# Gated recurrence: the merges of the blocks' inverses on GpSimd, with sums by halving additions

## The chip, the cores and the metric

The kernel runs on 1 core of one Trainium2 chip. The metric is the device time of one execution in microseconds (us); the time before is the median of 3 runs. The engines are TensorE (PE in the profile), VectorE (DVE), ScalarE (ACT), GpSimd (POOL) and SyncE (SP). Each runs its own list of instructions in order and waits for the others by semaphores.

## The reference

The program is a network of four layers with three sublayers each, on a state of 64 sequences x 32 steps x 128 features in float32. The change is in one sublayer, `_L1_attn_ref`, a gated recurrence with 16 heads of width 64:

```
def step(carry, inp):
    S, R = carry
    kn = k_t / max(norm(k_t), 1e-12)
    r = clip(v_t - S^T kn, -1, 1)
    S = a_t * S;   S = S + b_t * kn (v_t - S^T kn)^T
    o = S^T q_t
    R = aR_t * R;  R = R + g_t * kn (r - R^T kn)^T
    o = o + R^T q_t
```

`S` and `R` are 64 x 64 states for each sequence and head, `a`, `aR`, `b`, `g` are sigmoids of projections of the input, and the sequence has T = 32 steps. All `o` go through an output projection and are added to the state of the network.

## The kernel before

Twelve sublayers run one after the other (`program`, with a barrier between); `l1_attn` is the fifth of them. It doesn't step through time. For each sequence and head the recurrence is a triangular system over the 32 steps, I + L, with L built from products of keys, gates and betas. The kernel works on 16 tiles (`NT`) of 128 columns, 4 sequences x 32 steps each.

- TensorE builds the matrices of S and R in 5 levels (`fill_s`, `fill_r`, L3096). Between two levels VectorE scales rows and columns by the gates' products (`advance`, L3354 to L3362, operands in SBUF) and takes the results from PSUM by masked copies (`keep_s`, `keep_r`).
- The 32 x 32 system is inverted as two diagonal blocks of 16. ScalarE gathers the needed entries of `ms` and `mr` into `kc` (`gather`, L2927 and L2928). VectorE turns `kc` by 32 x 32 transposes into `lt` (`turn`, L3451), so that each partition holds one matrix, and sets the first off-diagonal of the inverse `xi` to minus that of `lt` (L3452). `merge(2)`, `merge(4)` and, for each of the two blocks of 16, `merge_last(n)` join pairs of inverted blocks: two batched small products, each an elementwise product into `tmp` with stride-0 and swapped operands (L3464, L3468, L3482, L3484) and a sum over the last axis (`tensor_reduce`, L3466, L3470, L3483, L3485). The minus sign sits in the second sum. `turn_back` (L3488) transposes `xi` back into `kc`, and ScalarE spreads it into `wideX` (`widen_x`).
- TensorE applies the inverses in a chain of steps per tile (`step_y`, `step_z`, `step_u`, `step_p`, `step_y2`, `step_z2`, `step_wr`, `step_o`, `step_out`), with copies by ScalarE between them; VectorE clips (`clip`, L3495) and adds the result (`result`, L3501).

The order on each engine is written out by hand in a loop of 18 rounds. In round i tile i is built (`now`), tile i-1 inverted (`mid`), tile i-2 applied (`old`) and tile i+1 projected (`new`). Round 1 has the first inversion and nothing to apply, round 16 the last inversion and no more building. In VectorE's list the pieces of the inversion stand among the levels: turn after the first advance, merge(2) after level 1 of S, merge(4) after level 1 of R, merge_last(0) after level 2, merge_last(1) after level 3, then `norms(i + 1)` (L3306 to L3308, which TensorE's `broadcast`, L3086, waits for), turn_back, the last level of S, and `keys(i + 1)`. In round 16 the order is turn, the merges with `result(13)` between merge(4) and merge_last, turn_back, clip. TensorE's `step_y(14)` waits for semaphore `x`, which `result(13)` raises. GpSimd does some memsets and the first residual of this sublayer and is idle for the rest of it.

`Steps` is a helper that lets an instruction raise a semaphore and its own engine wait for it before the next one.

## Time and profile before

| | |
|---|---|
| runs before, us | 3167.33 median (3166.45 to 3175.26) |
| profiled execution, us | 3174.15, span 3172.3 |
| TensorE busy | 2612.6 us (82%) |
| VectorE busy | 2138.2 us (67%) |
| ScalarE busy | 1425.9 us (45%) |
| GpSimd busy | 567.4 us (18%) |
| the sublayer, from its first fills to its last result | about 930 to 2066 us |

The profile is one execution. Busy time of an engine is the time in which an instruction of it ran. The view of waits says for each instruction how long its engine stood idle before it, and whose event ended that; "issue" is idle time for which the profile shows no releaser. The time in a row of the timeline is that of the whole merged group. Most of the span lies in other sublayers, which the change doesn't touch.

### The profile page before, as it was taken

How to read it: one execution, taken by the hardware profiler on the slowest of the kernel's cores; microseconds unless marked ns; L12 is line 12 of the kernel's file. 1: busy time of each engine (PE TensorE's matmuls, PEld its weight loads, DVE VectorE, ACT ScalarE, POOL GpSimd, SP SyncE). 2: the span in 40 equal slices, each digit the busy share in tenths (PEclk: the TensorE clock that was granted, in tenths of full speed). 3: DMA queues.
4: the chain of work that ended last, by engine and by line, in shares of the span. 5: the costliest groups of instructions: out<-in, count | busy, mean ns of one | idle time of the engine just before them, and what ended most of it. 6: DMA issues, size and time to landing. Idle time of an engine off the chain costs nothing. (4 is left out here: it accounts for less than half of the span.)

```text
span 3172.3 us, 120225 instructions
## 1 busy us (share of the span) xinstructions
PE 2612.6 (82%) x52165; PEld 1926.9 (61%) x52187; DVE 2138.2 (67%) x5457; ACT 1425.9 (45%) x3330; POOL 567.4 (18%) x592
## 2 busy tenths in 40 slices
PE   8977478999976788888888887769999997787735
PEld 5645365555656667676776776547776554575633
DVE  3348335777749889887988889267777666565742
ACT  4342233444453445444554443457776454464310
POOL 0000434555530000000000000010000441261025
PEclk9879687999988899999998999879999998798865
DMA  3200331111110000000000000000101003152013
GB/s 89 58 9 14 104 126 50 44 44 53 42 52 4 4 4 4 4 4 4 4 4 4 4 4 4 2 16 25 27 25 54 3 4 102 45 117 64 5 51 104
DMA packets 69932, 109.63 MB, mean 35 GB/s; under 512 B 10336, under 2 KB 55024, under 8 KB 68880
## 3 DMA queue, kind: packets, MB, share of 16 engines
q1 hardware_dynamic: 57776, 80.34, 8.0%
q0 software_dynamic: 11696, 22.40, 2.9%
q8 instruction: 382, 6.26, 0.8%
q14 instruction: 78, 0.64, 0.1%
HBM read 90.06 MB, written 16.51 MB: 34 GB/s over the span
## 5 line engine op out<-in xcount | busy, mean ns | idle before, releaser
L3096 PE MATMUL psum<-l1d_rw,l1d_cols 64*32 64x32 f32 (+2 forms) x20480 | 240.0, 215 | 85.9 <-issue 65.6
L3096 PEld LDWEIGHTS psum<-l1d_rw,l1d_cols 64*32 64x32 f32 x20480 | 209.3, 108 | 129.2 <-issue 104.1
L2476 POOL TENSOR_SCALAR l1xs_p<-l1xs_p,l1xs_col 128x257 f32<-128x257 f32 x256 | 233.8, 932 | 204.5 <-DVE l1xs_col L2432 204.5
L2397 ACT ACTIVATE l1xs_p<-psum,l1xs_col 128x257 f32<-128x257 f32 x256 | 119.5, 472 | 209.4 <-DVE l1xs_col L2427 203.1
L1747 POOL TENSOR_SCALAR X<-X,l1f_bias 128x512 f32<-128x512 f32 x4 | 6.3, 1589 | 1144.3 <-DMA l1f_bias<-in_l1f_bias 1144.3
L3354 DVE TENSOR_TENSOR l1d_rw<-l1d_rw,l1d_tots 128x1536 f32<-128x1536 f32 x96 | 143.2, 1491 | 72.6 <-PE psum L3096 71.6
L2870 ACT COPY l1d_ya<-psum 128x512 f32<-128x512 f32 x160 | 92.8, 590 | 197.9 <-PE psum L3136 196.7
L2439 DVE STREAM_TRANSPOSE l1xs_pt<-l1xs_p 128x288 f32<-128x288 f32 x256 | 122.4, 478 | 78.6 <-POOL l1xs_p L2476 78.5
L2692 ACT ACTIVATE l2x_p<-psum,l2x_top 128x257 f32<-128x257 f32 x256 | 120.5, 474 | 58.3 <-PE psum L2605 46.0
L3033 PE MATMUL psum<-l1d_src,l1d_wp 128*128 128x128 f32 x1024 | 138.5, 292 | 2.7 <-ACT l1d_src L2875 1.3
L2349 PE MATMUL psum<-l1xs_keys,l1xs_qx 128*32 128x257 f32 x2048 | 134.3, 396 | 3.5 <-DVE l1xs_qx L2421 1.9
L2361 PE MATMUL psum<-l1xs_pt,l1xs_vals 32*128 32x512 f32 x1152 | 136.6, 604 | 0.0
L3033 PEld LDWEIGHTS psum<-l1d_src,l1d_wp 128*128 128x128 f32 x1024 | 127.6, 203 | 7.0 <-issue 3.7
L2605 PE MATMUL psum<-consts,l2x_p 128*86 128x128 f32 x768 | 120.6, 280 | 1.7 <-ACT l2x_p L2692 1.1
L2734 DVE TENSOR_REDUCE l2x_top<-psum 128x1 f32<-128x257 f32 x256 | 96.9, 420 | 36.8 <-PE psum L2594 33.1
L1993 POOL TENSOR_TENSOR l2a_phi<-l2a_pos,l2a_ex 128x512 f32<-128x512 f32 x64 | 79.9, 1270 | 128.9 <-ACT l2a_ex L1979 128.9
L2427 DVE TENSOR_REDUCE l1xs_col<-psum 128x1 f32<-128x257 f32 x256 | 101.0, 409 | 2.7 <-PE psum L2349 2.6
L2605 PEld LDWEIGHTS psum<-consts,l2x_p 128*86 128x86 f32 x768 | 78.8, 122 | 33.4 <-issue 23.1
L3086 PE MATMUL psum<-l1d_small,l1d_hsel 32*128 32x384 f32 x256 | 67.0, 661 | 37.5 <-DVE l1d_small L3308 28.3
L2349 PEld LDWEIGHTS psum<-l1xs_keys,l1xs_qx 128*32 128x32 f32 x2048 | 61.9, 111 | 53.9 <-issue 24.7
L2330 PEld LDWEIGHTS psum<-XN,l1x_wqk 128*128 128x128 f32 x512 | 66.1, 202 | 46.9 <-issue 32.6
L2590 PE MATMUL psum<-l2x_keys,l2x_qx 32*128 32x257 f32 x512 | 90.1, 433 | 3.4 <-DMA l2x_mask<-l2x_table 3.4
(558 smaller groups left out, 6742.8 us busy)
## 6 DMA issues: line engine op xcount, KB each, us to landing
l2f_w<-in_l2f_w SPq DMA_DIRECT2D x16, 768.0 KB
l1xs_vals<-in_ctx_strips SPq DMA_DIRECT2D x16, 576.0 KB
l0x_ctxT<-in_ctxT SPq DMA_DIRECT2D x16, 516.0 KB, 3.7
l1xs_keys<-in_ctxT SPq DMA_DIRECT2D x16, 516.0 KB
l2x_ctxT<-in_ctxT SPq DMA_DIRECT2D x64, 129.0 KB, 2.1
l1d_wp<-in_l1d_wp SPq DMA_DIRECT2D x1, 2048.0 KB, 8.1
l2f_acc<-l2f_zero SPq DMA_DIRECT2D x8, 256.0 KB, 3.6
l2f_sums<-l2f_acc SPq DMA_DIRECT2D x8, 256.0 KB, 3.5
```

The lines of the kernel that those rows point to most:

```text
L2349: mm = nc.tensor.matmul(score_ps(t)[32 * c:32 * c + 32, :S2], qx[:, g % 2, n, 32 * c:32 * c + 32], keys[:, g % 2, c, :S2], start=True, sto ...
L2361: mm = nc.tensor.matmul(u_ps[c][:], vals[r, g % 2, j, :], pt[r, g % 2, :, j, :], start=(j == 0), stop=(j == STRIP - 1))
L2397: nc.scalar.activation(p[:, t % 4, :S2], score_ps(t)[:, :S2], ACT.Exp, bias=col[:, 0, t % 4:t % 4 + 1], accum_out=col[:, 1, t % 4:t % 4 + ...
L2427: nc.vector.tensor_reduce(col[:, 0, t % 4:t % 4 + 1], score_ps(t)[:, :S2], AX.X, ALU.max, negate=True).then_inc(s["mx"], 1)
L2439: nc.vector.transpose(pt[:, g % 2, n].rearrange("p j r -> p (j r)"), p[:, t % 4, :]).then_inc(s["pt"], 1)
L2476: nc.gpsimd.tensor_scalar(p[:, t % 4, :S2], p[:, t % 4, :S2], col[:, 2, t % 4:t % 4 + 1], None, ALU.mult).then_inc(s["norm"], 1)
L2605: mm = nc.tensor.transpose(t_ps[j % 2][:KC, c * 128:(c + 1) * 128], p[:, j, c * KC:(c + 1) * KC], k.const("ident"))
L2692: nc.scalar.activation(p[:, j, :S2], s_ps[j][:, :S2], ACT.Exp, bias=top[:, l % 2, j:j + 1], accum_out=sums[:, l % 2, j:j + 1]).then_inc(s[ ...
L2734: nc.vector.tensor_reduce(top[:, l % 2, j:j + 1], s_ps[j][:, :S2], AX.X, ALU.max, negate=True).then_inc(s["mx"], 1)
L3033: mm = nc.tensor.matmul(k.ps[into + j][:, e * 128:(e + 1) * 128], wp[:, n, c:c + 128], src[:], start=True, stop=True)
L3096: mm = nc.tensor.matmul(k.ps[bank0 + pr + e // per * 2][b * T:b * T + T, e % per * w:(e % per + 1) * w], cols[rr, 2 * n, e * 128 + b * T:e ...
L3354: tt(x, x, over.to_broadcast([128, feats.stop - feats.start, 32 * (16 >> lv), m]), ALU.mult)
```

## The change

The three merge functions move from VectorE's list to GpSimd's. GpSimd waits for `turn`, then does merge(2), merge(4) and merge_last for both blocks, whose instructions now alternate; two halves of `tmp` and of `wmat` keep the two blocks apart. Each `tensor_reduce` is replaced by additions that halve the last axis: one for 2, two for 4, three for 8 elements. The last addition of a merge writes straight into `xi`. The minus sign is taken in ScalarE's gathering: `kc` now holds the negated entries (`nc.scalar.mul` by -1.0 in place of `copy`), so the negated sums and the multiplication by -1 in `turn` fall away. `turn_back` waits for a new semaphore that GpSimd's last additions raise. The rest of VectorE's list keeps its order.

```
--- before.py
+++ after.py
@@ -2791,7 +2791,7 @@
     names = ("src", "srcv", "k_mm", "k", "q_mm", "q", "gate_mm", "gate", "nb_mm", "nb", "small", "bc_mm", "kn", "v_mm", "v",
              "rowS", "rowR", "mS_mm", "mS", "mR_mm", "mR", "kc", "back", "wideM", "wideX", "y_mm", "y", "z_mm", "t", "u_mm",
              "u", "p_mm", "r", "y2_mm", "y2", "z2_mm", "t2", "wr_mm", "wr", "o_mm", "o", "out_mm", "x", "zero", "diag",
-             "norm", "turn", "steps", "resid", "colr", "kr")
+             "norm", "turn", "steps", "resid", "colr", "kr", "merged", "last", "inverse")
     s = {n: k.sem("l1d_" + n) for n in names}
     with ph:
         sb = lambda n, shape, dt=F32: k.sb("l1d_" + n, shape, dt, ctx=ph)
@@ -2823,7 +2823,7 @@
         wideM, wideX = sb("wideM", [128, 5, H, 64]), sb("wideX", [128, 2 * H, 64])
         v, u, rd, ya = (sb(n, [128, 1024]) for n in ("v", "u", "rd", "ya"))
         kc, lt, xi = sb("kc", [128, T * T]), sb("lt", [128, T * (T + 1)]), sb("xi", [128, T * (T + 1)])
-        tmp, wmat = sb("tmp", [128, 1024]), sb("wmat", [128, 64])
+        tmp, wmat = sb("tmp", [128, 1024]), sb("wmat", [128, 128])
         block = ph.enter_context(nc.Block())
 
         def rows(first, last, lv):
@@ -2855,6 +2855,69 @@
             nc.gpsimd.memset(wideM[:], 0.0).then_inc(s["zero"], 1)
             pool.wait_ge(s["zero"], 2)
             nc.gpsimd.memset(xi[:, 0:T * T:T + 1], 1.0).then_inc(s["zero"], 1)
+            tt = nc.gpsimd.tensor_tensor
+
+            def blocks(x, m):
+
+                return (x.rearrange("p (n x) -> p n x", x=2 * m * (T + 1))[:, :, :2 * m * T]
+                        .rearrange("p n (r c) -> p n r c", c=T))
+
+            def merge(i, m):
+
+                nb, lb, xb = T // (2 * m), blocks(lt, m), blocks(xi, m)
+                lo, hi = slice(0, m), slice(m, 2 * m)
+                t5 = tmp[:, :nb * m * m * m].rearrange("p (n r c k) -> p n r c k", n=nb, r=m, c=m)
+                w4 = wmat[:, :nb * m * m].rearrange("p (n r c) -> p n r c", n=nb, r=m)
+                flat = tmp[:, :nb * m * m * m].rearrange("p (x k) -> p x k", k=m)
+                right = lambda x: x.rearrange("p n k c -> p n c k")
+                left = lambda x, r: x[:, :, r:r + 1, :].to_broadcast([128, nb, m, m])
+                step = Steps(pool, s["merged"], i, 10, {2: 0, 4: 4}[m])
+                for r in range(m):
+                    ins = tt(t5[:, :, r], left(lb[:, :, hi, lo], r), right(xb[:, :, lo, lo]), ALU.mult)
+                step(ins)
+                if m == 4:
+                    step(tt(flat[:, :, :2], flat[:, :, :2], flat[:, :, 2:], ALU.add))
+                step(tt(wmat[:, :nb * m * m], flat[:, :, 0], flat[:, :, 1], ALU.add))
+                for r in range(m):
+                    ins = tt(t5[:, :, r], left(xb[:, :, hi, hi], r), right(w4), ALU.mult)
+                step(ins)
+                if m == 4:
+                    step(tt(flat[:, :, :2], flat[:, :, :2], flat[:, :, 2:], ALU.add))
+                step(tt(xb[:, :, hi, lo], t5[:, :, :, :, 0], t5[:, :, :, :, 1], ALU.add))
+
+            def merge_last(i):
+
+                m = 8
+                lb, xb = blocks(lt, m), blocks(xi, m)
+                lo, hi = slice(0, m), slice(m, 2 * m)
+                w4 = [wmat[:, 64 * n:64 * n + 64].rearrange("p (r c) -> p r c", r=m) for n in range(2)]
+                t4 = [tmp[:, 512 * n:512 * n + 512].rearrange("p (r c k) -> p r c k", r=m, c=m) for n in range(2)]
+                flat = [tmp[:, 512 * n:512 * n + 512].rearrange("p (x k) -> p x k", k=m) for n in range(2)]
+                left = lambda x: x.unsqueeze(2).to_broadcast([128, m, m, m])
+                right = lambda x: x.rearrange("p k c -> p c k").unsqueeze(1).to_broadcast([128, m, m, m])
+                for part_ in range(8):
+                    for n in range(2):
+                        if part_ > 0:
+                            pool.wait_ge(s["last"], i * 14 + 2 * part_ + n - 1)
+                        if part_ == 0:
+                            ins = tt(t4[n], left(lb[:, n, hi, lo]), right(xb[:, n, lo, lo]), ALU.mult)
+                        elif part_ == 4:
+                            ins = tt(t4[n], left(xb[:, n, hi, hi]), right(w4[n]), ALU.mult)
+                        elif part_ in (1, 5):
+                            ins = tt(flat[n][:, :, :4], flat[n][:, :, :4], flat[n][:, :, 4:], ALU.add)
+                        elif part_ in (2, 6):
+                            ins = tt(flat[n][:, :, :2], flat[n][:, :, :2], flat[n][:, :, 2:4], ALU.add)
+                        elif part_ == 3:
+                            ins = tt(wmat[:, 64 * n:64 * n + 64], flat[n][:, :, 0], flat[n][:, :, 1], ALU.add)
+                        else:
+                            ins = tt(xb[:, n, hi, lo], t4[n][:, :, :, 0], t4[n][:, :, :, 1], ALU.add)
+                        ins.then_inc(s["inverse" if part_ == 7 else "last"], 1)
+
+            for i in range(NT):
+                pool.wait_ge(s["turn"], 2 * i + 2)
+                merge(i, 2)
+                merge(i, 4)
+                merge_last(i)
 
         @block.scalar
         def _(act):
@@ -2924,8 +2987,8 @@
                 if i > 0:
                     act.wait_ge(s["wideX"], i)
                 at = kc[:].rearrange("p (t c) -> p c t", t=T)
-                copy(at[:, :H, :], ms[:, i % 2, :, 0, :])
-                copy(at[:, H:, :], mr[:, i % 2, :, 1, :]).then_inc(s["kc"], 1)
+                nc.scalar.mul(at[:, :H, :], ms[:, i % 2, :, 0, :], -1.0)
+                nc.scalar.mul(at[:, H:, :], mr[:, i % 2, :, 1, :], -1.0).then_inc(s["kc"], 1)
 
             def widen(i, j):
 
@@ -3438,53 +3501,16 @@
                         ins = vc.copy_predicated(ll[:, i % 2, 1, hs[pr], :], top, part_[:, :, 1, :])
                 ins.then_inc(s["mR"], 1)
 
-            def blocks(x, m):
-
-                return (x.rearrange("p (n x) -> p n x", x=2 * m * (T + 1))[:, :, :2 * m * T]
-                        .rearrange("p n (r c) -> p n r c", c=T))
-
             def turn(i):
 
                 dve.wait_ge(s["kc"], i + 1)
                 t = Steps(dve, s["turn"], i, 2)
                 first = lambda x: x[:, T:T * T:2 * (T + 1)]
                 t(vc.transpose(lt[:, :T * T], kc[:]))
-                t(vc.tensor_scalar(first(xi), first(lt), -1.0, None, ALU.mult))
-
-            def merge(m):
-
-                nb, lb, xb = T // (2 * m), blocks(lt, m), blocks(xi, m)
-                lo, hi = slice(0, m), slice(m, 2 * m)
-                t5 = tmp[:, :nb * m * m * m].rearrange("p (n r c k) -> p n r c k", n=nb, r=m, c=m)
-                w4 = wmat[:, :nb * m * m].rearrange("p (n r c) -> p n r c", n=nb, r=m)
-                flat = tmp[:, :nb * m * m * m].rearrange("p (x k) -> p x k", k=m)
-                right = lambda x: x.rearrange("p n k c -> p n c k")
-                left = lambda x, r: x[:, :, r:r + 1, :].to_broadcast([128, nb, m, m])
-                for r in range(m):
-                    ins = tt(t5[:, :, r], left(lb[:, :, hi, lo], r), right(xb[:, :, lo, lo]), ALU.mult)
-                step(ins)
-                step(vc.tensor_reduce(wmat[:, :nb * m * m], flat, AX.X, ALU.add))
-                for r in range(m):
-                    ins = tt(t5[:, :, r], left(xb[:, :, hi, hi], r), right(w4), ALU.mult)
-                step(ins)
-                step(vc.tensor_reduce(wmat[:, :nb * m * m], flat, AX.X, ALU.add, negate=True))
-                step(vc.tensor_copy(xb[:, :, hi, lo], w4))
-
-            def merge_last(n):
-
-                m = 8
-                lb, xb = blocks(lt, m), blocks(xi, m)
-                lo, hi = slice(0, m), slice(m, 2 * m)
-                w4 = wmat[:, :m * m].rearrange("p (r c) -> p r c", r=m)
-                t4 = tmp[:, :512].rearrange("p (r c k) -> p r c k", r=m, c=m)
-                left = lambda x: x.unsqueeze(2).to_broadcast([128, m, m, m])
-                right = lambda x: x.rearrange("p k c -> p c k").unsqueeze(1).to_broadcast([128, m, m, m])
-                step(tt(t4, left(lb[:, n, hi, lo]), right(xb[:, n, lo, lo]), ALU.mult))
-                step(vc.tensor_reduce(w4, t4, AX.X, ALU.add))
-                step(tt(t4, left(xb[:, n, hi, hi]), right(w4), ALU.mult))
-                step(vc.tensor_reduce(xb[:, n, hi, lo], t4, AX.X, ALU.add, negate=True))
+                t(vc.tensor_copy(first(xi), first(lt)))
 
             def turn_back(i):
+                dve.wait_ge(s["inverse"], 2 * i + 2)
                 vc.transpose(kc[:], xi[:, :T * T]).then_inc(s["back"], 1)
 
             def clip(i):
@@ -3523,13 +3549,9 @@
                     advance_r(i, 0)
                     advance_s(i, 1)
                     keep_s(i, 1)
-                if mid:
-                    merge(2)
                 if now:
                     advance_r(i, 1)
                     keep_r(i, 1)
-                if mid:
-                    merge(4)
                 if i == NT:
                     result(i - 3)
                 if now:
@@ -3540,15 +3562,11 @@
                     keep_s(i, 2)
                     advance_r(i, 2)
                     keep_r(i, 2)
-                if mid:
-                    merge_last(0)
                 if now:
                     advance_s(i, 3)
                     keep_s(i, 3)
                     advance_r(i, 3)
                     keep_r(i, 3)
-                if mid:
-                    merge_last(1)
                 if new:
                     norms(i + 1)
                 if mid:
```

## Rows read from the trace of the kernel before

**Rows 1.** Busy time by stretch (columns in its first line, x = instructions)
```profile
core 0: us, PE busy (x) PEld busy (x) DVE busy (x) ACT busy (x) POOL busy (x), PEclk, DMA share, GB/s
1003.00:1068.00 65.00, 40.94 (x1596) 32.82 (x1598) 63.63 (x131) 26.51 (x53) 0.00 (x0) 0.82 0.01 3
...
1390.00:1455.00 65.00, 55.97 (x1987) 45.59 (x1987) 56.88 (x119) 31.23 (x62) 0.00 (x0) 0.92 0.02 4
```

**Rows 2.** Who waited for whom, TensorE, 1130 to 1910 us
```profile
PE psum L3096 <- issue: 41.6, 43, 2.2
...
PE psum L3086 <- DVE l1d_small L3308: 17.2, 11, 2.2
```

**Rows 3.** The same view and stretch, VectorE
```profile
DVE l1d_rw L3354 <- PE psum L3096: 57.5, 41, 3.7
```

**Rows 4.** One stretch, instructions on tile tmp alone
```profile
1399.60:1442.80 43.20, 10.49 (x24) 1.00 0.02 4
```

**Rows 5.** Groups of instructions on GpSimd, all of the span
```profile
L2476 POOL TENSOR_SCALAR l1xs_p<-l1xs_p,l1xs_col 128x257 f32<-128x257 f32 x256 | 233.8, 932 | 204.5 <-DVE l1xs_col L2432 204.5
...
L1993 POOL TENSOR_TENSOR l2a_phi<-l2a_pos,l2a_ex 128x512 f32<-128x512 f32 x64 | 79.9, 1270 | 128.9 <-ACT l2a_ex L1979 128.9
...
L2552 POOL TENSOR_TENSOR l2x_qx<-l2x_q,consts 128x128 f32<-128x128 f32 x64 | 25.5, 398 | 330.6 <-PE psum L2594 294.4 <-DVE l2x_q L2727 36.2
...
L2857 POOL MEMSET l1d_xi<- 128x32 f32 x1 | 0.2, 154 | 0.1
```

**Rows 6.** In order of time, VectorE, one middle tile; start us, us, then instruction
```profile
1399.45 0.18 DVE L3452 TENSOR_SCALAR l1d_xi<-l1d_lt 128x16 f32<-128x16 f32 x1
...
1441.19 0.23 DVE L3306 TENSOR_SCALAR l1d_small<-l1d_small 128x128 f32<-128x128 f32 x1
...
1442.78 1.24 DVE L3488 STREAM_TRANSPOSE l1d_kc<-l1d_xi 128x1024 f32<-128x1024 f32 x1
```

**Rows 7.** The same stretch as rows 4, line L3354 alone
```profile
1399.60:1442.80 43.20, 10.19 (x7) 1.00 0.02 4
```

**Rows 8.** The same stretch, line L3356 alone
```profile
1399.60:1442.80 43.20, 4.77 (x7) 1.00 0.02 4
```

**Rows 9.** The page's costliest groups
```profile
L2870 ACT COPY l1d_ya<-psum 128x512 f32<-128x512 f32 x160 | 92.8, 590 | 197.9 <-PE psum L3136 196.7
...
L3086 PE MATMUL psum<-l1d_small,l1d_hsel 32*128 32x384 f32 x256 | 67.0, 661 | 37.5 <-DVE l1d_small L3308 28.3
```

**Rows 10.** Who waited for whom, TensorE, 930 to 1003 us
```profile
PE psum L3086 <- DVE l1d_small L3308: 3.0, 2, 2.5
```

**Rows 11.** The same view, 1003 to 1068 us
```profile
PE psum L3086 <- DVE l1d_small L3308: 6.1, 1, 6.1
```

**Rows 12.** In order of time, ScalarE, middle tile
```profile
1439.45 0.28 ACT L2918 ACTIVATE l1d_small<-psum 128x128 f32<-128x128 f32 x1
```

**Rows 13.** In order of time, TensorE, middle tile
```profile
1437.42 2.08 PE L3136 MATMUL psum<-l1d_ya,l1d_wideX 64*64 64x64 f32 x64
...
1441.38 0.36 PE L3096 MATMUL psum<-l1d_rw,l1d_cols 64*32 64x48 f32 x21 [0.76 <-issue]
...
1442.92 1.52 PE L3086 MATMUL psum<-l1d_small,l1d_hsel 32*128 32x384 f32 x8 [1.18 <-DVE l1d_small L3308]
```

**Rows 14.** In order of time, VectorE, the last tile
```profile
1993.12 0.18 DVE L3452 TENSOR_SCALAR l1d_xi<-l1d_lt 128x16 f32<-128x16 f32 x1
...
1997.56 0.29 DVE L3501 TENSOR_TENSOR X<-X,psum 128x128 f32<-128x128 f32 x1
...
2014.88 0.69 DVE L3495 TENSOR_SCALAR l1d_rd<-psum 128x512 f32<-128x512 f32 x1 [8.59 <-PE psum L3136]
```

**Rows 15.** In order of time, TensorE, the last tile
```profile
1997.94 3.68 PE L3136 MATMUL psum<-l1d_v,l1d_wideX 64*64 64x64 f32 x64 [5.85 <-issue]
```

**Rows 16.** Groups of instructions on ScalarE, all of the span
```profile
L2927 ACT COPY l1d_kc<-l1d_ms 128x512 f32<-128x512 f32 x16 | 18.0, 1124 | 0.0
...
L620 ACT ACTIVATE l0a_sc<-psum 128x512 f32<-128x512 f32 x16 | 8.6, 610 | 6.5 <-PE psum L527 6.5
```


## The prediction

> **What bounds the kernel now.** The change touches one stage of twelve, the gated recurrence, which runs from about 930 to 2066 us of the span; all else keeps its time. I read the stage in this order: busy time by stretch, who waits for whom, one tile in order of time, and then the two ends of the loop.
>
> The windows show two regimes. In the tile 1003 to 1068 us VectorE is busy 63.6 of 65 us and TensorE 40.9, so VectorE sets the pace. In a tile of the middle both are near the top, TensorE 56.0 and VectorE 56.9 of 65 [rows 1]. Busy shares alone don't say which of two engines leads; the waits do. Over 1130 to 1910 us VectorE waited 57.5 us at L3354 for TensorE's fills [rows 3], while TensorE's waits that name VectorE are led by 17.2 us for the key norms (`small`, L3308) [rows 2]. TensorE's largest idle is the 41.6 us "issue" in the fills, gaps in the middle of a run of matmuls that no engine caused [rows 2]. So TensorE leads in the middle tiles, VectorE runs just behind it, and a lighter VectorE can give back only those places where TensorE stands waiting for it.
>
> **The merges leave VectorE.** In the middle tile the instructions that touch `tmp` took 10.5 us [rows 4]; with the two copies into `xi` and the hand-offs I take 11 us a tile (estimate). This is the most that a tile can win, and only where VectorE leads.
>
> **The merges on GpSimd.** Per tile, from the diff: merge(2) has 6 instructions of 32 elements; merge(4) 10 of 64 and 2 of 128; merge_last 4 each of 512, 256, 128 and 64. GpSimd's tensor_tensor took 1270 ns for 512 elements and 398 ns for 128 [rows 5]. The line through both is 108 ns + 2.27 ns an element, which gives 181 ns for 32, 253 for 64, 689 for 256. The sum is 1.1 + 3.3 + 10.4 = 14.8 us. Some 24 of the 34 instructions wait for the one before; the one such wait in the trace cost 0.1 us (last column of the memset L2857) [rows 5], so 2.4 us more: 17.3 us from turn to last merge. The rows have no strided or broadcast operand on GpSimd. As an upper bound I take its dearest rate per element, 932 ns for 257 [rows 5], 3.2 ns, and 0.3 us a wait: 20 + 7 = 27 us. As a lower bound, 15 us. I take 17.3, because the nearest row is the same operation.
>
> Is it hidden? In the middle tile `turn` ends at 1399.63 and `turn_back`, which now waits for GpSimd, starts at 1442.78 [rows 6]. It would start at about 1441.4 (below), so 41.7 us are free. What stands behind turn_back on VectorE is the last take of S, the next tile's keys, and behind these TensorE's broadcasts: a late GpSimd would stop everything. At 17 or 27 us it isn't late.
>
> **Both engines at once.** No row shows a GpSimd operation beside a VectorE operation with two SBUF inputs; I bound it. At best nothing. At worst one holds the other off for each whole instruction. VectorE's `advance` lines with two SBUF inputs take 10.2 and 4.8 us between turn and turn_back [rows 7, 8]. Added whole to GpSimd's chain that is 17.3 + 15.0 = 32.3 us, still under 41.7. VectorE would in turn wait for remains of GpSimd instructions, on average under 0.5 us each for 14 advances and fewer while GpSimd is busy: 0 to 6 us a tile. In the middle tiles this has cover: 11 us of merges are gone, and VectorE waited for the fills anyway. In the tile where VectorE leads it counts. I take 5 us there.
> The Trainium skill, "SBUF — State Buffer", section "Who interferes with whom", speaks against the change: a VectorE instruction with two SBUF inputs and a GpSimd instruction that reads SBUF take turns on one read interface, and the one that comes later is blocked for the whole instruction. By that rule the worst case above is the true one, with the sum as I give it; without it the tile that VectorE leads would win 5 us more. No row of before has both kinds side by side.
>
> **Middle tiles: the wait for the norms.** The page has 28.3 us of TensorE waiting at L3086 for `small` [rows 9]; 3.0 us of it lie before the first merge [rows 10] and 6.1 in the VectorE-led tile [rows 11], which leaves 19.2 us for 13 tiles. In the tile shown, ScalarE's square root ended at 1439.73 [rows 12], but VectorE began the norms only at 1441.19, after merge_last [rows 6]. Without the merge the norms begin 1.46 us earlier. TensorE waited 1.18 us [rows 13], so here all goes. In tiles without an issue gap ahead of it the wait was longer and a remainder stays, since ScalarE and the norms alone outlast TensorE's 2.08 us of step_wr and its fill: about 0.5 us, the tiles without merges show the same kind. So 19.2 - 13 x 0.5 = 12.7 us. What is late next is TensorE's own "issue" gap, as the 0.76 us before this very wait [rows 13]: if instructions are what comes late, a removed wait in part becomes such a gap. I take off 2.7: **10 us** (bounds 0 to 19).
>
> **The VectorE-led tile.** 11 us leave VectorE, contention returns 5: **6 us** (bounds 0 to 11). TensorE allows it: it waited 6.1 us there for the norms [rows 11] and its 40.9 us busy leave room [rows 1]. The tile after it may give 1.
>
> **The last tile.** Here GpSimd's chain is bare. Before, VectorE ends turn at 1993.30, does merge(2) and merge(4), and only then `result` at 1997.56 [rows 14]; TensorE's next step starts at 1997.94 after 5.85 us of idle that the profile calls issue, but step_y waits for just this result (`x`) [rows 15]. After the change result follows turn at once: 4.2 us earlier. But the clip that TensorE needs later (2014.88) now stands behind turn_back, and that behind GpSimd: 1993.3 + 17.3 + 1.25 for the transpose = 2011.9. So the end moves by 2014.88 - 2011.9 = **3 us** (bounds +4 to -7, the latter for a chain of 27).
>
> **ScalarE's sign and the rest: 0.** The gathering copy of 512 elements took 1124 ns [rows 16], strided in its output; the same multiply by a constant took 610 ns dense [rows 16], where the dense COPY took 590 (ya, on the page) [rows 9]. 20 ns each is nothing, ends +-0.2 us a tile, and it lies ahead of turn with room except once at the end. tensor_copy for tensor_scalar on 16 elements: 0. The third wait of `turn_back` costs what is said above.
>
> Sum: 10 + 6 + 1 + 3 = 20 us. The profiled execution took 3174.15 us (span 3172.3), so 3154 for its like. That execution lies 6.8 us above the median of 3167.33, and the same 20 us off the median give **3147 us**.
>
> **Rivals.**
> *A, the supply of instructions rules (chance 0.2).* For: 41.6 us of issue gaps, the largest wait of TensorE, in nearly every tile. Against: in most tiles no gap follows the norms. Then the 10 us shrink to 2 and the led tile gives 3; with the 3 at the end, 8 us: 3159, no change that can be told.
> *B, GpSimd is late for turn_back (0.1), the other sign.* It decides once chain plus contention passes 41.7 us; from there each microsecond costs one in each of 14 tiles. For: nothing shows GpSimd's rate on broadcast, strided operands. At its upper bound, 27 + 15 = 42 us, it only just decides; at 45 (a chain of 30) it costs 3.3 x 14 = 46, and at the bare end 30 - 20.3 = 10 more, with the norms' gain kept (10): 3167 + 46 = 3213. Against: the chain would have to be 1.6 times mine, with all the contention on top.
> *C, more comes free (0.12).* No contention, so the led tile gives 11, the norms 15, and the shorter idle at the end lets the step there, 3.68 us [rows 15], take the 2.08 of the same step in the middle tile [rows 13]: some 32 us with 1 of the tile after the led one: 3135.
> *D, nothing is freed in the led tile and the chain is 25 us (0.08).* VectorE is slowed by as much as it was relieved: 10 + 0 - 5 = 5 us: 3162.
> The forecast holds the remaining 0.5.
>
> **Numbers.** About 0.3%, 9.5 us, is what can be told from no change. Faster by more: forecast (most of it) and C and a part of A: 0.66. Within: rest of A, D: 0.22. Slower: B and the worst of D: 0.12. Range 3126 to 3174, which holds A, C and D, with the far end of B outside. The profiled executions may scatter as the runs before did (3166.45 to 3175.26).
>
> **What would show it.** The lines of the merges stand under POOL with about 17 us a tile, 240 to 280 us in all, 512-element products near 1.27 us alone; above 1.4 us beside VectorE they are held off. The advances' mean (1.75 us for 1536 elements in the trace of before) grows if VectorE is held off. TensorE's wait for `small` falls from 28 to about 10 us, VectorE's busy in the middle tile from 57 to about 46, and its waits for TensorE rise by as much. VectorE's wait at turn_back is nil but in the last tile, where it is 15 us or more. If the issue gaps grow by what the wait for `small` lost, A is right; if turn_back waits in the middle tiles, B. Wrong altogether: TensorE's idle in the middle tiles unchanged with a lighter VectorE, or a stage longer than before.

## The result, and the profile after

The changed kernel takes 3152.41 us (median of 15 runs, 3136.83 to 3166.28) and the kernel before, run between them on the same chip, 3169.91 us (15 runs, 3157.01 to 3187.12). The ratio, taken between neighbouring runs and not between the two medians, is 0.9936 with a 95% interval of 0.9914 to 0.9958: 20.3 us faster by the ratio, 17.5 between the medians. Forecast were 20 us and 3147 us, with a range of 3126 to 3174; the 3147 stood on a median of 3167.33 from three runs, which fifteen runs put 2.6 us higher. The profiled execution took 3154.11 us, its span 3152.2 us.

The page's first row (busy time, share of the span, instructions) says what moved: GpSimd 567.4 us before, 957.4 after; VectorE 2138.2 before, 2044.7 after.

```profile
PE 2617.1 (83%) x52187; PEld 1929.1 (61%) x52187; DVE 2044.7 (65%) x5041; ACT 1426.2 (45%) x3330; POOL 957.4 (30%) x1136
```

390 us came to GpSimd and only 93.5 left VectorE. The rest of this text is about that disproportion and about where the 20 us lie.

The stage from its first `turn` to its last `result` took 1057.3 us before and 1038.5 after: 18.8 us less. I cut it at the starts of the turns: the led tile (the one in which VectorE leads, first to second turn), the next tile, the middle (third to fifteenth turn, 12 tiles), the tile ahead of the end, and the end (last turn to last result). The windows of the kernel before, with the columns of [rows 1], led tile and middle:

```profile
1007.80:1065.20 57.40, 36.69 (x1405) 29.00 (x1406) 56.13 (x117) 24.61 (x49) 0.00 (x0) 0.79 0.01 3
1135.20:1937.35 802.15, 688.35 (x23831) 560.72 (x23826) 698.69 (x1430) 386.05 (x741) 0.00 (x0) 0.93 0.02 4
```

The kernel after: led tile, middle, and one middle tile that answers to the second of [rows 1]:

```profile
1009.40:1063.40 54.00, 36.66 (x1405) 29.11 (x1406) 52.04 (x92) 24.64 (x49) 27.33 (x34) 0.84 0.02 4
1130.46:1918.74 788.28, 679.25 (x23831) 555.32 (x23826) 630.02 (x1117) 386.36 (x741) 296.35 (x408) 0.95 0.02 4
1389.00:1454.00 65.00, 57.08 (x1995) 46.69 (x1995) 53.51 (x95) 32.98 (x64) 24.82 (x34) 0.95 0.02 4
```

Led tile 57.4 to 54.0, middle 802.15 to 788.28, and over the middle VectorE's busy 698.69 to 630.02. TensorE's own busy time fell as well, 688.35 to 679.25, at a granted clock of .93 before and .95 after, although its matmuls are the same. The waits of TensorE in the middle, before (waiting line, releaser, sum in us, times, longest; the lines are the fills, the broadcast that waits for the norms, and the steps):

```profile
PE psum L3096 <- issue: 41.6, 43, 2.2
PE psum L3086 <- DVE l1d_small L3308: 18.7, 12, 2.2
...
PE psum L3136 <- issue: 6.6, 10, 1.1
```

and after:

```profile
PE psum L3159 <- issue: 52.5, 51, 2.5
...
PE psum L3199 <- issue: 7.6, 13, 1.3
...
PE psum L3149 <- DVE l1d_small L3371: 3.8, 6, 0.7
```

The wait for the norms fell from 18.7 to 3.8 us, and the issue gaps of fills and steps together rose from 48.2 to 60.1. Last, two groups of VectorE's waits in the stage after: its largest, for TensorE's fills at the advances (71.6 us before), and a new one, for GpSimd at `turn_back`:

```profile
DVE l1d_rw L3417 <- PE psum L3159: 112.7, 51, 5.7
...
DVE l1d_kc L3514 <- POOL l1d_xi L2913: 16.4, 1, 16.4
```

### The profile page after: what moved, and what is told of

It reads as the page before. It is cut to its first block and busy times, and to the rows that moved or that the text cites. A ratio compares the mean times of both kernels' runs of the same rounds, so it can differ in the third digit from the quotient of the medians.

```text
span 3152.2 us, 120361 instructions
## 1 busy us (share of the span) xinstructions
PE 2617.1 (83%) x52187; PEld 1929.1 (61%) x52187; DVE 2044.7 (65%) x5041; ACT 1426.2 (45%) x3330; POOL 957.4 (30%) x1136
## 5 line engine op out<-in xcount | busy, mean ns | idle before, releaser
L2876 POOL TENSOR_TENSOR l1d_tmp<-l1d_lt,l1d_xi 128x64 f32<-128x64 f32 (+1 forms) x96 | 41.7, 463 | 666.0 <-DVE l1d_xi L3510 664.7
L3417 DVE TENSOR_TENSOR l1d_rw<-l1d_rw,l1d_tots 128x1536 f32<-128x1536 f32 x96 | 168.2, 1753 | 112.8 <-PE psum L3159 112.7
L2439 DVE STREAM_TRANSPOSE l1xs_pt<-l1xs_p 128x288 f32<-128x288 f32 x256 | 122.4, 478 | 78.6 <-POOL l1xs_p L2476 78.6
L2552 POOL TENSOR_TENSOR l2x_qx<-l2x_q,consts 128x128 f32<-128x128 f32 x64 | 25.4, 398 | 329.0 <-PE psum L2594 293.9
L3419 DVE TENSOR_TENSOR l1d_cols<-l1d_cols,l1d_tots 128x512 f32<-128x512 f32 x96 | 96.3, 1004 | 0.0
```

Source lines behind the costliest of these rows:

```text
L2439: nc.vector.transpose(pt[:, g % 2, n].rearrange("p j r -> p (j r)"), p[:, t % 4, :]).then_inc(s["pt"], 1)
L3417: tt(x, x, over.to_broadcast([128, feats.stop - feats.start, 32 * (16 >> lv), m]), ALU.mult)
```

## Experiments

Each was run beside the kernel before, whose median was 3173.3 to 3174.4 us in the three groups. Stretches are read from one trace each, and the traced run can lie some way off the median of its kernel (last column of the table below). x1 is the changed kernel once more, so that traces of the same program can be set side by side: how far apart two of them lie bounds what one stretch can tell.

**x1, the changed kernel again.** No edit.

> The changed kernel once more, as the measure for the others of this chip. My theory (TensorE leads, VectorE's merges held up the norms): 20 us under the kernel before, ratio 0.993 to 0.995.

Measured: 3152.96 us, ratio 0.9936 [0.9912, 0.9959]. Led tile 55.3 (54.0 in the first trace), middle 793.33 (788.28), end 72.5 (73.0). The time repeats; the middle scatters by 5 us between these two traces. x4 and x6 change nothing in TensorE's list for the middle, which took 792.9 and 780.8 us there: two single traces of the same middle can lie 12 us apart. The kernel before has one trace, with 802.2 us. That the middle gained doesn't rest on one pair: the eight traces with at most 7 us of waits for the norms and turn_back not late lie at 778.5 to 793.3, all under it, and the two with more work ahead of the norms (x9, x10) at 817.1 and 819.0. x3 and x8 repeat the led tile of before (57.3 and 57.5 for 57.4), x3 and x10 its end (71.2 and 73.3 for 73.2), so the end is good to 2 us.

**x2, no merges at all.**
```diff
-            for i in range(NT):
-                pool.wait_ge(s["turn"], 2 * i + 2)
-                merge(i, 2)
-                merge(i, 4)
-                merge_last(i)
...
-                dve.wait_ge(s["inverse"], 2 * i + 2)
```

> The changed kernel without any merge on GpSimd and without turn_back's wait for it (the inverses are left out, the output is not the reference's). This is the change with neither contention nor a bare chain at the end. Theory: contention costs only where VectorE leads, so the first inverted tile gives 3 to 5 us more than the changed kernel's, the middle tiles nothing, the last tile about 6 (no wait for GpSimd, so no idle of TensorE before step_y2): 9 us under the changed kernel, VectorE's advances back at 1757 and 685 ns. Rival (contention is paid in all tiles): 4.6 us a tile, 50 us or more under the changed kernel.

Measured: 3143.61 us, 0.9918 [0.9891, 0.9945]. The windows of its led tile and middle:

```profile
1009.65:1060.20 50.55, 35.55 (x1405) 28.64 (x1406) 46.13 (x92) 24.69 (x49) 0.00 (x0) 0.86 0.02 4
1126.54:1905.01 778.47, 672.22 (x23864) 551.81 (x23856) 576.46 (x1118) 387.27 (x743) 0.00 (x0) 0.96 0.02 4
```

VectorE's busy time in the led tile is 46.13 us, with the merges on GpSimd it was 52.04, in the same 92 instructions: GpSimd's presence costs VectorE 5.9 us there. The led tile is 3.5 us shorter than in the changed kernel (4.7 than in x1) and the end 7 us. The middle is 10 (15) us shorter, but this is the trace of the fastest of six runs, 16.5 us under their median, and only 2 us shorter than the middle of x6. The medians of x1 and x2 lie 9.3 us apart, and 9 was expected: that little is left to win from the merges, wherever they run.

**x3, no GpSimd: merge_last(1) on VectorE, but ahead of the last advances.** From the kernel before:
```diff
                 if mid:
                     merge_last(0)
+                    merge_last(1)
                 if now:
                     advance_s(i, 3)
...
-                if mid:
-                    merge_last(1)
                 if new:
                     norms(i + 1)
```

> The kernel before, all merges on VectorE, with merge_last(1) moved from after level 3 to right after merge_last(0), so that nothing of the inversion stands ahead of the norms. Theory: the middle tiles' gain is TensorE's wait for the norms alone, so this gets it with no GpSimd at all: the wait for the norms falls from 28 to about 15 us (the led tile keeps its part), 10 us under the kernel before. Rival (what counts is VectorE's total load): no change, since VectorE does the same work.

Measured: 3155.51 us, 0.9941 [0.9919, 0.9964]. VectorE does the same work as before; only its last 3.6 us of merging no longer stand right ahead of the norms. TensorE's waits in the middle:

```profile
PE psum L3096 <- issue: 51.1, 48, 2.5
...
PE psum L3086 <- DVE l1d_small L3308: 4.1, 7, 0.7
```

The wait for the norms goes from 18.7 to 4.1 us and the middle from 802.15 to 790.61, what the whole change reached (788.28 and 793.33). The led tile stays at 57.3. The whole run is 18.9 us under the kernel before where I had expected 10, and x1 21.4, a difference that the intervals don't tell apart. So the gain in the middle comes from where VectorE's work stands and not from the engine that does it.

**x4, clip ahead of turn_back in the last round.** From the changed kernel:
```diff
+                if i == NT:
+                    clip(i - 2)
                 if mid:
                     turn_back(i - 1)
-                if i == NT:
-                    clip(i - 2)
```

> The changed kernel with the clip of tile 14 ahead of the last turn_back, so that it doesn't wait for GpSimd's bare chain. Theory: the clip comes 3.1 us earlier, TensorE's 4.5 us of idle before step_y2 shrinks to about 1.3, and the two steps behind it take 2.1 and 2.0 us in place of 3.7 and 3.8: 6 us under the changed kernel, seen between the last turn and the last result (73.0 before, 67 now). Rival (the end is bound by ScalarE's copies or the matmuls themselves): 0 to 3 us.

Measured: 3148.69 us, 0.9924 [0.9899, 0.995], 4.3 us under x1 by the medians, which the intervals don't tell apart; the end took 65.5 us against 73.0 and 72.5, 7 us less where 6 were expected. VectorE at the end of the changed kernel (start, duration, wait in brackets):

```profile
1976.20 0.18 DVE L3510 COPY l1d_xi<-l1d_lt 128x16 f32<-128x16 f32 x1
...
1993.55 1.25 DVE L3514 STREAM_TRANSPOSE l1d_kc<-l1d_xi 128x1024 f32<-128x1024 f32 x1 [16.43 <-POOL l1d_xi L2913]
1994.71 1.25 DVE L3521 TENSOR_SCALAR l1d_rd<-psum 128x512 f32<-128x512 f32 x2
```

and in x4:

```profile
1995.55 0.69 DVE L3521 TENSOR_SCALAR l1d_rd<-psum 128x512 f32<-128x512 f32 x1 [13.54 <-PE psum L3199]
1996.48 0.69 DVE L3521 TENSOR_SCALAR l1d_rd<-psum 128x512 f32<-128x512 f32 x1 [0.24 <-PE psum L3199]
1998.86 1.25 DVE L3514 STREAM_TRANSPOSE l1d_kc<-l1d_xi 128x1024 f32<-128x1024 f32 x1 [1.69 <-POOL l1d_xi L2913]
```

The clip no longer stands behind the 16.4 us wait for GpSimd, and turn_back itself waits 1.69 us. TensorE's steps on this path in the kernel before:

```profile
2002.39 3.75 PE L3131 MATMUL psum<-l1d_v,consts 128*128 128x512 f32 x4 [0.77 <-ACT l1d_ya L2870]
...
2016.56 2.08 PE L3136 MATMUL psum<-l1d_rd,l1d_wideX 64*64 64x64 f32 x64 [0.79 <-DVE l1d_rd L3495]
2019.41 1.96 PE L3131 MATMUL psum<-l1d_rd,consts 128*128 128x512 f32 x4 [0.78 <-ACT l1d_ya L2870]
```

in the changed kernel:

```profile
1977.21 2.08 PE L3199 MATMUL psum<-l1d_v,l1d_wideX 64*64 64x64 f32 x64 [0.50 <-issue]
...
1996.02 3.68 PE L3199 MATMUL psum<-l1d_rd,l1d_wideX 64*64 64x64 f32 x64 [4.48 <-DVE l1d_rd L3521]
2000.47 3.75 PE L3194 MATMUL psum<-l1d_rd,consts 128*128 128x512 f32 x4 [0.78 <-ACT l1d_ya L2933]
```

and in x4:

```profile
1997.23 2.08 PE L3199 MATMUL psum<-l1d_rd,l1d_wideX 64*64 64x64 f32 x64 [0.80 <-DVE l1d_rd L3521]
2000.09 1.96 PE L3194 MATMUL psum<-l1d_rd,consts 128*128 128x512 f32 x4 [0.78 <-ACT l1d_ya L2933]
```

The two steps behind the clip take 2.08 and 1.96 us before and in x4, 3.68 and 3.75 us in the changed kernel, where TensorE had stood idle for 4.48 us ahead of them. The windows of the changed kernel around its first and second row above have the granted clock behind the five busy times, 1.00 and then 0.50, that is 2.4 and 1.2 GHz:

```profile
1977.00:1979.50 2.50, 2.08 (x64) 1.97 (x64) 0.11 (x1) 0.75 (x2) 2.17 (x9) 1.00 0.03 7
...
1995.90:1999.80 3.90, 3.68 (x64) 3.49 (x64) 0.06 (x1) 0.64 (x2) 0.00 (x0) 0.50 0.02 4
```

So 3.4 us hung on the idle time, besides the wait itself. The price isn't fixed. Behind the same wait the two steps took 3.21 and 3.67 us in x1 (idle 4.62) and 3.68 and 1.95 in x9 (idle 4.90): the first step paid each time, the second not always. In the kernel before, it was paid at the head of this path, at 1997.94 [rows 15] and 2002.39 (3.68 and 3.75 us); in x3, with 5.84 us of idle at the same place, it was 3.61 and 1.96.

**x5, GpSimd busy, but only writing.** From the changed kernel, in place of the merges:
```diff
-                merge(i, 2)
-                merge(i, 4)
-                merge_last(i)
+                step = Steps(pool, s["last"], i, 25)
+                for n in range(25):
+                    step(nc.gpsimd.memset(tmp[:], 0.0))
+                nc.gpsimd.memset(tmp[:], 0.0).then_inc(s["inverse"], 2)
```

> The changed kernel with 26 memsets of tmp per tile on GpSimd (about 27 us, each waiting for the one before) in place of the merges (which are left out). GpSimd is as busy as in the changed kernel but only writes. Theory (the two engines contend for reading): VectorE's advances are back at the durations of before, 1757 ns for 1536 elements and 685 ns for 512, and the memsets stay at 0.95 us. Rival (any GpSimd work slows VectorE): the 512-element advances stay near 1000 ns.

Measured: 3165.02 us (one run), led tile 53.2, middle 789.93; the end took 80.1 us, since the last tile waits for 26 us of memsets in place of 17 us of merges. VectorE's two-input advances in the whole stage (group, count, sum, mean ns; these two in x5):

```profile
L3418 DVE TENSOR_TENSOR l1d_rw<-l1d_rw,l1d_tots 128x1536 f32<-128x1536 f32 x48 | 84.4, 1757 | 86.1 <-PE psum L3160 86.0
L3420 DVE TENSOR_TENSOR l1d_cols<-l1d_cols,l1d_tots 128x512 f32<-128x512 f32 x96 | 65.8, 685 | 0.0
```

The same in the kernel before (the 1536 group took 1757 ns there too, `COPY_PREDICATED` is the masked copy from PSUM):

```profile
L3356 DVE TENSOR_TENSOR l1d_cols<-l1d_cols,l1d_tots 128x512 f32<-128x512 f32 x96 | 65.8, 685 | 0.0
L3405 DVE COPY_PREDICATED l1d_ms<-l1d_lmask,psum 128x384 f32<-128x384 int32 x96 | 62.9, 722 | 0.0
L3354 DVE TENSOR_TENSOR l1d_rw<-l1d_rw,l1d_tots 128x1024 f32<-128x1024 f32 x48 | 58.8, 1226 | 59.8 <-PE psum L3096 59.4
```

and in the changed kernel:

```profile
L3419 DVE TENSOR_TENSOR l1d_cols<-l1d_cols,l1d_tots 128x512 f32<-128x512 f32 x96 | 96.3, 1004 | 0.0
L3417 DVE TENSOR_TENSOR l1d_rw<-l1d_rw,l1d_tots 128x1536 f32<-128x1536 f32 x48 | 90.8, 1892 | 53.7 <-PE psum L3159 53.7
L3417 DVE TENSOR_TENSOR l1d_rw<-l1d_rw,l1d_tots 128x1024 f32<-128x1024 f32 x48 | 77.4, 1613 | 59.2 <-PE psum L3159 59.0
L3468 DVE COPY_PREDICATED l1d_ms<-l1d_lmask,psum 128x384 f32<-128x384 int32 x96 | 63.1, 724 | 0.0
```

With 26 memsets of 953 ns a tile on GpSimd the advances take what they take with GpSimd idle. With products on GpSimd 512 elements take 1004 ns in place of 685, 1024 take 1613 in place of 1226, 1536 take 1892 in place of 1757, and the masked copies, which read PSUM, 724 in place of 722. So GpSimd's writing costs VectorE nothing here, and what the merges do beyond it, reading, holds VectorE off, in instructions with two operands in SBUF and not in the masked copies. That is the rule of the Trainium skill, "SBUF — State Buffer", section "Who interferes with whom", and these rows agree with it. Single rows spread widely: of the 96 advances of 512 elements in the changed kernel the shortest took 680 ns, the median 789 and the longest 2039. The longest comes near 685 ns and a whole product of 1.5 us; that one always waits out the other to its end isn't shown.

**x6 and x7, a longer chain on GpSimd.** From the changed kernel, with a spare tile:
```diff
                 pool.wait_ge(s["turn"], 2 * i + 2)
+                step = Steps(pool, s["spare"], i, 4)   # x7: 12
+                for _ in range(4):                     # x7: 12
+                    step(tt(spare[:], lt[:, :512], lt[:, 512:1024], ALU.mult))
                 merge(i, 2)
```

> The changed kernel with 4 more products of 512 elements per tile on GpSimd, ahead of the merges, each waited for: 6.4 us bare, about 8 with contention. Theory: the chain of 28 us has 41.7 us of room in the middle tiles, so their pitch doesn't change; the last tile pays 6.4 us and the half-speed steps stay, the first inverted tile pays about 3: 9 us over the changed kernel, ratio about 0.997. Rival (GpSimd's chain is already what turn_back waits for): 8 us in each of 16 tiles, 120 us more.

> The same with 12 more products, 19 us bare and some 22 with contention: a chain of about 50 us against 41.7 us of room. Theory: turn_back now waits for GpSimd by 5 to 8 us in each middle tile, 75 to 110 us in all, and 19 us at the end. This puts a price on the point from which the change would have been a loss. Rival (room is larger, since turn_back's followers have slack of their own): the waits show but the pitch grows by less than half of them.

Measured: x6 3160.93 us, 0.9958 [0.9938, 0.9977]; x7 3207.24 us (one run), 54 more than the changed kernel. In x6 the middle took 780.8 us, the led tile 55.9, the end 78.6: nothing is lost but at the bare end, 6 us of the 8 by which the median lies above x1 (9 expected). In x7 the middle took 813.1, the led tile 66.5 and the end 87.2, and VectorE waited for GpSimd in ten tiles:

```profile
DVE l1d_kc L3518 <- POOL l1d_xi L2914: 51.6, 10, 32.8
```

32.8 us of this lie in the last tile and 18.8 in the nine others, of which six are in the middle, with 9.0 us. There turn_back starts again and again 44.9 us after turn ends, the length of GpSimd's chain, and the waits are 0.5 to 2.5 us. So the room is 42 to 44 us, as [rows 6] gave (41.7). I had expected 75 to 110 us for the middle, from a chain of 50 us; the chain was 44.8 us long, and the middle lost 20 to 25. Of these the waits at turn_back explain less than half. VectorE was busy 705 us, 75 more than in the changed kernel, and TensorE now waited 20.8 us for its masked copies.

**x8, x3 with the end put right, no GpSimd.**
```diff
                 if mid:
                     turn(i - 1)
+                if i == NT:
+                    result(i - 3)
...
+                if i == NT:
+                    clip(i - 2)
                 if mid:
                     turn_back(i - 1)
```
(on top of x3; both are taken out where they stood).

> The kernel before with nothing on GpSimd: merge_last(1) right after merge_last(0) as in the run before, and in the last round result(13) right after turn and the clip ahead of turn_back. Theory: the middle tiles keep the 11 us of that reordering, the end goes from 73 to 66 us, the first inverted tile stays at 57.5: 18 us under the kernel before, as much as the change itself gives. Rival (GpSimd is needed for most of the gain): under 10 us.

Measured: 3153.68 us, 0.9921 [0.989, 0.9952], 19.8 us under the kernel before by the medians (18 expected); the end took 68.9 us, 2.3 to 4.4 less than in the three traces without its edits, where 7 were expected. TensorE there:

```profile
1985.21 2.60 PE L3224 MATMUL psum<-l1d_rd,l1d_wo 128*128 128x128 f32 x16 [2.72 <-ACT l1d_v L2870]
1988.86 3.68 PE L3136 MATMUL psum<-l1d_v,l1d_wideX 64*64 64x64 f32 x64 [1.04 <-issue]
1993.30 3.65 PE L3131 MATMUL psum<-l1d_v,consts 128*128 128x512 f32 x4 [0.77 <-ACT l1d_ya L2870]
```

Here the steps take 3.68 and 3.65 us where they can take 2.08 and 1.96. Ahead of them stand idles of 2.72 and 1.04 us. In x1 the first of them took 2.08 us behind idles of 2.70 and 0.50, in x6 2.94 behind 2.69 and 0.50, so these rows give no idle time from which it begins; this end still pays at its head.

**x9, VectorE loaded again, just ahead of the norms.** From the changed kernel:
```diff
                     keep_r(i, 3)
+                if mid and i < NT:
+                    for _ in range(7):
+                        step(vc.memset(spare[:], 0.0))
```

> The changed kernel with seven memsets of 512 elements (485 ns each, 3.5 us) on VectorE, at the place where merge_last(1) stood, ahead of the norms. They only write, so they don't hold off GpSimd. VectorE still has 7.5 us a tile less than before the change. Theory (only what stands ahead of the norms counts in the middle tiles): TensorE's wait for the norms in the middle goes from 4 back to about 18 us, and the middle tiles lose their gain of 11 us: ratio 0.997 (first tile and end keep theirs). Rival (VectorE's total load counts): a third of the gain lost, 0.995, and the wait stays under 8 us.

Measured: 3184.53 us, 1.0037 [1.0013, 1.0061]: 31.6 us over x1 and 11.3 over the kernel before, where I had expected the gain of the middle to go and the rest to stay (0.997). The seven memsets took 4.5 us a tile, not 3.5, because each waited 0.17 us for the one before, and the wait for the norms came to 27.6 us and not 18. The middle, with VectorE's busy time third:

```profile
1137.72:1954.83 817.11, 695.82 (x23831) 566.40 (x23828) 669.08 (x1202) 386.60 (x741) 296.64 (x408) 0.91 0.02 4
```

```profile
PE psum L3160 <- issue: 41.3, 41, 2.4
PE psum L3150 <- DVE l1d_small L3372: 27.6, 12, 3.2
```

This is the plainest of the experiments. VectorE is busy 669 us here, 30 less than in the kernel before, and yet the middle is 15 us longer: 817.11 against 802.15. Its total load isn't what counts here, but the 4.5 us (before 3.6) that stand between the last advance and the norms.

**x10, the new arithmetic on the old engine.** From the kernel before: halving additions for each tensor_reduce, the sign taken by ScalarE, merges left on VectorE.
```diff
                 step(tt(t4, left(lb[:, n, hi, lo]), right(xb[:, n, lo, lo]), ALU.mult))
-                step(vc.tensor_reduce(w4, t4, AX.X, ALU.add))
+                flat = tmp[:, :512].rearrange("p (x k) -> p x k", k=m)
+                halve(flat, m)
+                step(tt(wmat[:, :m * m], flat[:, :, 0], flat[:, :, 1], ALU.add))
```
(halve adds the upper half of the last axis to the lower until two elements are left; the other sums likewise).

> The kernel before with the other two parts of the change alone: sums by halving additions and the sign taken by ScalarE, all merges still on VectorE. Expected by both: a reduction of 512 elements, 686 ns, becomes additions of 256, 128 and 64 of together about 1 us, and the copies into xi go; VectorE gets about 1.2 us a tile more. Theory: half of that stands ahead of the norms, about 0.3 us in each of 13 tiles, and 1 us in the first: 3 to 6 us slower than before, no change that can be told. Rival (halving or the sign is a gain by itself): 5 us or more under the kernel before.

Measured: 3185.94 us, 1.0044 [1.002, 1.0067]. One merge_last takes 4.37 us against 3.63, and TensorE in the middle:

```profile
PE psum L3096 <- issue: 42.5, 47, 2.4
PE psum L3086 <- DVE l1d_small L3308: 26.0, 12, 3.0
```

0.74 us more ahead of the norms, and the wait for them goes from 18.7 to 26.0: 7.3 us over 12 tiles, 0.61 a tile. Its cost, 12.7 us by the medians and 14 by the ratio, is above the 3 to 6 that I expected: those left out that TensorE's busy time would be longer too, by 11.5 us at a granted clock of .91.

The middle of all traces (us; "norms" is TensorE's wait for `small`, "issue" its issue gaps in fills and steps; "trace" is how far the traced run lies above the median of its kernel):

| | middle | norms | issue | PE busy | clock | led tile | end | trace |
|---|---|---|---|---|---|---|---|---|
| before | 802.2 | 18.7 | 48.2 | 688.4 | .93 | 57.4 | 73.2 | +4.2 |
| changed | 788.3 | 3.8 | 60.1 | 679.3 | .95 | 54.0 | 73.0 | +1.7 |
| x1 | 793.3 | 4.5 | 55.5 | 686.8 | .94 | 55.3 | 72.5 | +14.3 |
| x2 | 778.5 | 4.5 | 54.6 | 672.2 | .96 | 50.6 | 65.6 | -16.5 |
| x3 | 790.6 | 4.1 | 58.7 | 679.2 | .95 | 57.3 | 71.2 | +8.1 |
| x4 | 792.9 | 3.9 | 60.5 | 685.0 | .94 | 56.6 | 65.5 | +3.2 |
| x5 | 789.9 | 4.5 | 61.2 | 675.4 | .95 | 53.2 | 80.1 | one run |
| x6 | 780.8 | 4.5 | 52.8 | 676.9 | .95 | 55.9 | 78.6 | -10.7 |
| x7 | 813.1 | 6.6 | 46.7 | 690.7 | .93 | 66.5 | 87.2 | one run |
| x8 | 788.1 | 4.4 | 57.6 | 681.1 | .94 | 57.5 | 68.9 | +4.9 |
| x9 | 817.1 | 27.6 | 48.2 | 695.8 | .91 | 58.4 | 71.3 | -2.9 |
| x10 | 819.0 | 26.0 | 49.8 | 699.9 | .91 | 60.2 | 73.3 | +7.6 |

## Why the prediction was right, step by step

**The sum was right; three of its four terms were not quite.** 10 + 6 + 1 + 3 was forecast. The two traces of the changed kernel give 14 and 9 in the middle, 3.4 and 2.1 in the led tile, 2.9 and 2.3 in the next, 0.2 and 0.7 at the end: 20 and 14 in all. The tile ahead of the end took 1.7 and 0.3 us more, so the whole stage gave 18.8 and 13.6, where the ratio of the runs gives 20.3 and the medians 17.5 and 21.4. That the total came out so close is in part luck: led tile and end gave 5 to 6 us less than forecast, and the next tile and, in the first trace, the middle gave as much more.

**Middle tiles: mechanism right, make-up mis-sized.** The norms' wait fell by 14.9 us where I had 12.7. "What is late next is TensorE's own issue gap" holds too, and I took off 2.7 for it where the gaps grew by 12 (x1: 7). That is rival A's mechanism, at A's size in the first trace (four fifths of what the norms lost) and at half of what they lost in x1; A's outcome, 2 us for the middle, didn't come. What I had not put in is TensorE's busy time, which fell as well. In three traces of the changed middle (changed, x1, x4) it fell by 9.1, 1.6 and 3.4 us, and TensorE's whole idle time by 4.8, 7.3 and 5.9. Between traces of the same work the busy time scatters by as much as it fell, so how much of the gain is fewer waits and how much is a higher granted clock (.93 before, .94 to .95 after) stays open. x9 and x10 show the same terms the other way round: norms up, issue at its old size, clock .91, busy time up by 7 and 12 us. That the clock follows from the waits is argued from such rows; no run changed the one and held the other. Why an issue gap comes in where a wait went stays open too: the rows before and after only name it "issue".

**The merges leave VectorE: right size, wrong credit.** VectorE's busy time in the middle fell by 5.7 us a tile: 10.2 us of merges (698.7 before, 576.5 in x2, over 12 tiles), where I had 11 with the hand-offs, less 4.5 of contention. The sign that I gave, 57 to about 46 us in the middle tile, left the contention out; it was 53.5. But x3 shows that the middle would have had its gain with the merges still on VectorE, and x9 that VectorE lighter by 30 us is slower if the work stands ahead of the norms. My own step said this ("the norms begin 1.46 us earlier") and I then told the change as an unloading. The unloading as such is worth the led tile, some 2 us, and no more: with GpSimd and without it, x1 (0.9936) and x3 (0.9941), then x4 (0.9924) and x8 (0.9921), are pairs that the intervals don't tell apart.

**The led tile: 6 forecast, 3.4 and 2.1 measured.** VectorE's busy time fell from 56.1 to 52.0, 10.0 us of merges less 5.9 of contention by x2 (11 and 5 forecast), so 4.1 and not 6 were there to win. TensorE takes the rest: its busy time in this tile depends on the clock, 36.7 us at .84 in the changed kernel, 40.6 at .73 in x4, where the tile took 56.6 us (0.8 us less than before). "TensorE allows it" was a little too good.

**The chain on GpSimd: 17.3 forecast, 17.05 measured.** Bare, in the last tile (start, duration, us; the third row ends the chain at 1993.51):

```profile
1976.46 0.47 POOL L2876 TENSOR_TENSOR l1d_tmp<-l1d_lt,l1d_xi 128x32 f32<-128x32 f32 x2 [30.07 <-DVE l1d_xi L3510]
...
1982.43 3.00 POOL L2903 TENSOR_TENSOR l1d_tmp<-l1d_lt,l1d_xi 128x512 f32<-128x512 f32 x2
...
1992.96 0.55 POOL L2913 TENSOR_TENSOR l1d_xi<-l1d_tmp 128x64 f32<-128x64 f32 x2
```

The parts were off in both directions: the two broadcast products took 1.50 us each where I took 1.27 from a dense row, so that the sign "above 1.4 us" could not tell contention from a slower operand; and only the 10 waits of merge(2) and merge(4) cost anything, 0.08 us each, since the two halves of merge_last take turns. Beside VectorE the chain took 25.6 us in a middle tile (24.6 to 26.3) and 28.2 in the led one; the bound was 32.3. Its groups there (count, sum, mean ns):

```profile
L2905 POOL TENSOR_TENSOR l1d_tmp<-l1d_xi,l1d_wmat 128x512 f32<-128x512 f32 x32 | 59.8, 1891 | 0.0
L2903 POOL TENSOR_TENSOR l1d_tmp<-l1d_lt,l1d_xi 128x512 f32<-128x512 f32 x32 | 57.1, 1808 | 1.3
```

A 512-element product takes 1.81 to 1.89 us in the mean against 1.50 bare. GpSimd is busy 24.4 us a tile, not 17: the 240 to 280 us that I forecast for its lines left out its own share of the contention, and 390 was measured.

**Contention: the rule held, its cost was hidden.** All advances together grew by 74 us, 4.6 a tile, in the range of 0 to 6. In the middle it fell on time in which VectorE would have waited for the fills: x5, with neither merges on VectorE nor contention, took 789.9 us there, the changed kernel 788.3 and 793.3. Rival C, which had no contention, is out in its first condition.

**The last tile: the wait as forecast, the gain not.** The clip came 3.2 us earlier relative to turn (23.0 before, 19.8 after), as worked out. The end moved 0.2 and 0.7 us. The step that failed is that an earlier clip is passed on whole. The step behind it did start 3.6 us earlier (21.1 us after turn, 24.7 before), but at half the clock: `result` had freed TensorE early, its steps ran at 2.08 us, were done by 1991.5, and it then idled 4.48 us. The time that rival C had seen at the head (3.4 us: 2.08 and 1.96 us there in place of 3.68 and 3.75) was gained and lost again behind the clip, on the path, as x4 shows by taking the idle away. I had the row for this ([rows 15], 3.68 us after an idle) and used it only for rival C. I also took the clip for what was late before; its 8.59 us of waiting for TensorE [rows 14] say that TensorE led there.

**Rival B** didn't come: turn_back waits once, for 16.4 us (15 or more forecast). x7 moved it into reach and shows where it decides, at 42 to 44 us. With a chain of 44.8 us the stage without its end took 34 to 40 us more than in the changed kernel's two traces; the price that I gave, one microsecond for one in each of 14 tiles past 41.7, makes 43. It is near, but in good part for another reason, VectorE's contention and not the wait. ScalarE's sign cost nothing: its two halves 1136 and 1145 ns against 1124 and 1149 for the copies.

**What is best.** x4 (3148.69) and x8 (3153.68) lie at 0.9924 and 0.9921 against the kernel before, both a little under the change's 0.9936, by less than the intervals tell apart. That x8 needs no GpSimd at all is the more telling of the two. x2 puts the floor, without any merges, at 0.9918 [0.9891, 0.9945].

## What to carry to other kernels

When the leading engine waits for another at one place, look at what stands directly ahead of that place in the other's order: moving 3.6 us of work from there gained here as much as moving 11 us a tile to an idle engine, and putting 4.5 us there cost some 31 us though VectorE stayed lighter than it had been. Price a move to GpSimd by the traffic between the two engines (here GpSimd's chain stretched from 17 to 26 us and VectorE's advances by 8 to 47% in the mean), and price every idle of TensorE by the steps that follow it too.

## What the runs showed of the hardware

- GpSimd's tensor_tensor with a broadcast and a strided operand took 1.50 us for 512 elements, against 1.27 us dense, and 0.235 us for 32.
- VectorE was held off by GpSimd's products and additions in instructions with two SBUF operands (685 to 1004 ns for 512 elements), not by memsets of 953 ns each (685 ns in x5), and not in masked copies from PSUM (722 and 724 ns).
- The same TensorE step took 2.08 us after an idle of 0.50, 0.80 or 1.65 us (changed, x4, x9) and 3.68, 3.21 and 3.68 after one of 4.48, 4.62 and 4.90 (changed, x1, x9); the next one took 3.75, 3.67 and 1.95, against 1.96. In the changed kernel the granted clock was 1.00 and 0.50 in the two steps compared. In x8 the slow steps followed idles of 2.72 and 1.04 us, one shortly after the other.
- TensorE's issue gaps in fills and steps went up from 48 to 60 us over twelve tiles (x1: 56) when its waits for the norms went down from 19 to 4, and stood at 48 and 50 where these waits were 28 and 26 us.
